# A gated cross-attention block with a ternary feed-forward layer: VectorE makes the second half's gated product before the sum of the exponentials

## The reference

```
h   = layernorm(x)
x   = x + tanh(g_xattn) * (softmax((h Wq)(ctx Wk)^T / 8) (ctx Wv) Wo + bo)      # 8 heads of 64
h   = layernorm(x)
g, u = bitlinear(h, w_gate), bitlinear(h, w_up)                                 # 512 -> 2048
x   = x + tanh(g_ffn) * bitlinear(relu(g)^2 * u, w_down)                        # 2048 -> 512
bitlinear(a, w) = act_quant(a) @ weight_quant(w).T
   act_quant: each row is scaled to 127 / max|row| and rounded; weight_quant: ternary, -1, 0 or 1 times a mean
```

## Time and profile before

| what | value |
|---|---|
| median of 3 runs | 1203.57 us (1203.33 to 1204.34) |
| the profiled execution: its own time | 1205.63 us |
| its span in the trace | 1203.7 us |
| granted TensorE clock over the span (1 is full speed) | 0.997 |
| TensorE busy with matrix products | 1181.2 us, 98% |
| VectorE busy | 1029.0 us, 85% |
| ScalarE busy | 870.7 us, 72% |
| GpSimd busy | 307.4 us, 26% |

### The profile page before, as it was taken

The page is one execution under the profiler, slowest core; times in us unless marked ns, Lnnn a source line. Parts: engine busy times, 40 slices in busy tenths (PEclk is TensorE's granted clock), DMA queues, the critical chain, the costliest instruction groups (busy, mean ns, idle before and its releaser), DMA issues.

```text
span 1203.7 us, 18706 instructions
## 1 busy us (share of the span) xinstructions
PE 1181.2 (98%) x5859; PEld 743.6 (62%) x5859; DVE 1029.0 (85%) x2123; ACT 870.7 (72%) x928; POOL 307.4 (26%) x313
## 2 busy tenths in 40 slices
PE   9998999999999999999999999999999999999997
PEld 7655566656656666666556656666665666566653
DVE  4888888888989888888988888889898888888876
ACT  4877767777877777677877766776787777677764
POOL 3231222222442222222432222222244222222200
PEclk9998999999999999999999999999999999999999
DMA  9796445444444464344444445444444444444432
GB/s 341 267 288 162 101 99 101 114 100 98 96 105 101 104 186 108 93 104 106 100 98 96 116 147 136 97 109 97 106 100 100 98 99 115 100 98 96 98 66 58
DMA packets 286268, 144.60 MB, mean 120 GB/s; under 512 B 254509, under 2 KB 254893, under 8 KB 283684
## 3 DMA queue, kind: packets, MB, share of 16 engines
q1 hardware_dynamic: 286240, 144.32, 47.0%
q10 hardware_dynamic: 4, 0.00, 0.0%
HBM read 57.86 MB, written 24.35 MB: 68 GB/s over the span
## 4 chain that ended last, share of the span: by engine, by line
PE 77%; DVE 11%; ACT 5%; issue 4%; DMA 3%; SPq 0%; POOL 0%; DVEq 0%; ACTq 0%; POOLq 0%
PE gu_ps L1000 30%; PE o_ps L970 16%; PE s_ps L66 14%; PE y_ps L1014 14%; DVE half_max L1249 2%; DVE staged L1243 2%; DMA v_scr<-x 2%; DMA w_down<-in_wu_t 1%; ACT x_marked L811 1%; DVE probs L1221 1%; DVE prob_sum L1225 1%; ACT v_sb L672 1%; PE gu_ps L1060 1%; ACT staged L785 1%; DVE stats L1278 1%
## 5 line engine op out<-in xcount | busy, mean ns | idle before, releaser
L1000 PE MATMUL gu_ps<-w_gate,xq_t 128*128 128x512 bf16 x1016 | 242.6, 382 | 12.5 <-DVE staged L1243 11.5
L1000 PE MATMUL gu_ps<-w_up,xq_t 128*128 128x512 bf16 x1024 | 242.5, 380 | 0.0
L1014 PE MATMUL y_ps<-w_down,hq_t 128*128 128x512 bf16 x1008 | 228.0, 379 | 1.4 <-DMA hq_t<-staged 1.3
L970 PE MATMUL o_ps<-v_sb,pt_high 128*128 128x512 f32 (+1 forms) x640 | 212.8, 413 | 0.0
L1243 DVE TENSOR_TENSOR staged<-staged,gu_ps 128x1024 f32<-128x1024 f32 x128 | 155.6, 1215 | 61.1 <-ACT staged L748 61.1
L66 PE MATMUL s_ps<-a_sb,xf_high 128*128 128x308 f32 x1024 | 187.3, 305 | 0.0
L610 POOL TENSOR_TENSOR rstd<-var_eps,neg_half 128x1 f32<-128x1 f32 x128 | 96.3, 752 | 310.6 <-DVE var_eps L1208 271.4
L1000 PEld LDWEIGHTS gu_ps<-w_up,xq_t 128*128 128x128 bf16 x1024 | 100.2, 98 | 121.8 <-issue 1.3
L1014 PEld LDWEIGHTS y_ps<-w_down,hq_t 128*128 128x128 bf16 x1008 | 98.3, 98 | 121.0 <-DMA hq_t<-staged 1.8
L1000 PEld LDWEIGHTS gu_ps<-w_gate,xq_t 128*128 128x128 bf16 x1016 | 94.0, 98 | 127.1 <-issue 15.9
L785 ACT ACTIVATE staged<-staged,h_scale 128x1024 f32<-128x1024 f32 x126 | 138.1, 1144 | 46.8 <-DVE h_scale L1263 46.5
(11 more groups left out here) (142 smaller groups left out, 1438.5 us busy)
## 6 DMA issues: line engine op xcount, KB each, us to landing
xf_sb<-in_x_feat SPq DMA_DIRECT2D x64, 256.0 KB, 2.7
x_sb<-in_x_tok SPq DMA_DIRECT2D x64, 256.0 KB, 2.9
y<-staged SPq DMA_DIRECT2D x64, 256.0 KB, 2.1
staged<-in_wg_t SPq DMA_DIRECT2D x4, 1024.0 KB, 9.8
staged<-in_wd_t SPq DMA_DIRECT2D x4, 1024.0 KB, 7.3
folded<-a_scr SPq DMA_DIRECT2D x3, 1232.0 KB, 5.6
v_scr<-x SPq DMA_DIRECT2D x12, 256.0 KB, 2.7
folded<-v_scr SPq DMA_DIRECT2D x3, 1024.0 KB, 7.7
```

The lines of the kernel that those rows point to most:

```text
L970: last = nc.tensor.matmul(o_ps[:, :], pt[0:rows, P * c:P * (c + 1)], v_sb[0:rows, v, c, :], start=(c == 0 and pt is pt_high and v == 0), s ...
L1000: last = nc.tensor.matmul(target[:, q, :], xq_t[:, s.par(0), c, :], w[:, c, cols], start=(c == 0), stop=(c == DC - 1))
L1014: last = nc.tensor.matmul(y_ps[:, :], hq_t[:, c, :], w_down[:, c, :], start=(c == 0), stop=(c == FC - 1))
```

## The change

In VectorE's `step`, `hidden_half(s, 1)` of tile t moves ahead of `sum_probs(s, 3)` of tile t+3. `top_half(s, 1)` and `hidden_scales` stay behind the sum. Nothing is added or removed.

```diff
                     if s.has(1):
                         hidden_unit_scale(s, 1)
+                    if s.has(0):
+                        hidden_half(s, 1)
                     if s.has(3):
                         sum_probs(s, 3)
                     if s.has(0):
-                        hidden_half(s, 1)
                         top_half(s, 1)
                         hidden_scales(s)
```

## The result

The changed kernel takes 1223.25 us (median of 5 runs, 1222.87 to 1224.94), the kernel before 1204.34 beside it (5 runs, 1203.33 to 1206.17). The ratio is 1.015, 95% interval 1.0138 to 1.0161: slower, by some 19 us. Forecast were 1220.4, and 1208 to 1230. TensorE is busy as long as before (1181.2 us there), and so it is idle longer.

What follows compares the result with a forecast made beforehand. TensorE, 17.28 us per tile, was taken as the bound; the free engines' loop becomes 16.84 - 0.65 + 1.27 = 17.46 and overtakes it. With first, split, load and end terms, 1203.57 + 16.8 = 1220.4 us, range 1208 to 1230.

Steps and rivals of the forecast that it cites:

- first interval: From the second-half product of tile 0 to the next tile's: 18.5 us, with tile 0's product 0.94 earlier.
- three value tiles, over the loop: Tiles where GpSimd splits the values: each 2.44 us over the free loop, on ScalarE's mark-to-shift path, 7.3 in all.
- three key tiles: Tiles where GpSimd splits the keys after a later `normalise`: scores about 0.9 us late, some 0.65 passed on, 2.0 in all.
- two load tiles: Tiles falling on the next batch's loads, where the planes' transpose comes late: 2.6 us for both, between 1 and 4.5.
- The loop of 16.84: The kernel before: time per tile through VectorE and ScalarE running freely, 0.44 us under TensorE's 17.28.
- The longer part: From second-half product to `mark_hidden`, which now waits behind ScalarE's planes: 4.66 us instead of 3.39, so 1.27 longer.
- The shorter part: From `shift_scores` to second-half product, which now waits for ScalarE's square: 2.69 us instead of 3.34, a gain of 0.65.
- TensorE's waits: At `attend` (L970), TensorE waits for `pt_low` (L1232), moved back 0.82 us against the product, in most tiles.
- The rule weighed: GpSimd and VectorE lock a shared SBUF port: `xq` costs 0.86 us more per value tile; mere sharing would give 1217.8.
- TensorE as the bound: Rival: the new loop stays under TensorE's 17.28 us per tile, about 1208.5 us in all; chance 0.06.
- the planes in time: Rival: ScalarE's planes are not late, `mark_hidden` comes at 4.22, loop 17.02, no change at 1203.5 us; chance 0.05.
- the steeper one: Rival: sum and `mark_hidden` start only after product and planes fully end; loop 17.69, 1234.0 us; chance 0.07.

Runs made afterwards that it cites:

- experiment 11: The changed kernel unaltered, measured again beside other runs on one chip: 1224.01 us, ratio 1.0157 to the kernel before.
- The first experiment: The changed kernel with GpSimd's `normalise` multiplying only the first of each head's 77 exponentials: 1211.22 us, ratio 1.005 to the kernel before.
- The third: The kernel before with the second-half product moved ahead of the sum in every second step only: 1210.78 us, ratio 1.0048.
- The sixth experiment: The changed kernel with `hidden_unit_scale` moved a step later, into VectorE's gap ahead of the first-half product: 1226.99 us, ratio 1.0185 to the kernel before.
- experiments 4: The kernel before with the three one-element instructions of `hidden_unit_scale` moved behind `hidden_scales`: 1212.3 us, ratio 1.0056.
- the seventh: The changed kernel with the sum moved further, behind `top_half` and `hidden_scales`: 1388.28 us, ratio 1.1525 to the kernel before.
- 8: The changed kernel with GpSimd splitting all five value chunks ahead of `normalise` instead of three: 1227.35 us, ratio 1.0184 to the kernel before.

## Why the prediction was right

The forecast of 1220.4 stands 2.9 below the median. Its steps against the changed kernel's trace, where both counted from the product of tile 0 to that of tile 60:

| step of the prediction | forecast | measured |
|---|---|---|
| sum, inverse, `normalise`, planes, `mark_hidden` after the product | 1.13, 1.95, 2.23, 3.48, 4.66 | 1.14, 1.96, 2.24, 3.49, 4.67 |
| ordinary interval | 17.46 | 17.43 (17.51 at every fourth) |
| first interval | 18.5 | 18.02 |
| three value tiles, over the loop | 2.44 each | 2.4 each |
| three key tiles | 0.65 each | 1.1 each |
| two load tiles | 2.6 | 0.8 (1.3 in experiment 11) |
| tile behind a value tile | none | 0.7 each |
| 60 intervals | 1060.5 | 1061.0 |
| behind tile 60 | 0.7 | 16.35 - 15.64 = 0.71 |

**One reading of the kernel before was too wide.** The loop of 16.84 was said to hold no instruction that waits for TensorE. VectorE's rows hold none, but ScalarE's relu of the second half did wait (timeline of ScalarE in the kernel before):

```profile
643.82 1.03 ACT L742 ACTIVATE staged<-gu_ps 128x1024 f32<-128x1024 f32 x1 [0.60 <-PE gu_ps L1000]
```

The 16.84 stands all the same: the square behind that relu ended at 646.49, and the product at 647.03 came straight behind the sum's inverse, with no idle time ahead of it.

**The longer part** is the step on which it all rested, and it held to 0.01 us. The first experiment shows the planes as its cause and not only their company. The third shows the threshold.

**The shorter part** was right too: the product waits for ScalarE's square, here 0.18 us where I expected some 0.3, and the distance from the shift to the product is 529.08 - 526.40 = 2.68, forecast 2.69. The sixth experiment shows that time freed on VectorE ahead of the product is worth nothing.

**Every fourth interval** is 0.08 longer. The trace says where: at the border of two rounds of four steps ScalarE's planes start 1.33 us after `normalise` and not 1.25 (timeline of ScalarE; `normalise` started at 513.81).

```profile
515.14 1.27 ACT L755 ACTIVATE planes<-probs 128x1280 int16<-128x1280 int16 x1 [3.60 <-POOL probs L615]
```

The kernel before has the same 0.08 at the same tiles, where it costs nothing. That it is the loop's branch is likely from its place, and not shown. Some 13 times 0.08 is 1.0 us which the prediction didn't have, and its 17.46 instead of 17.43 covered it.

**The key tiles** were sized too small, 0.65 against 1.1. The scores wait, and relu behind them, in the timelines of TensorE and ScalarE:

```profile
325.78 0.83 PE L66 MATMUL s_ps<-a_sb,xf_high 128*128 128x308 f32 x4 [1.00 <-POOL a_sb L598]
```

```profile
331.23 1.02 ACT L742 ACTIVATE staged<-gu_ps 128x1024 f32<-128x1024 f32 x1 [1.55 <-PE gu_ps L1000]
```

GpSimd started on the keys when it was expected, 318.78 - 315.37 = 3.41 after the product, but took 6.94 us for them, where the prediction carried over 6.49 (timelines of GpSimd, over all of it and over its end):

```profile
318.78 6.94 POOL L598 TENSOR_TENSOR a_sb<-folded,a_sb 128x616 fp32r<-128x616 f32 x4
```

```profile
323.76 1.96 POOL L598 TENSOR_TENSOR a_sb<-folded,a_sb 128x616 fp32r<-128x616 f32 x1
```

Each of its four instructions takes 1.5 us alone, and the one that meets `pt_low` takes 2.1, in both kernels. The fourth (the second row) took 1.96 instead of 1.53: VectorE's `unmark_hidden` now comes while the third is at work and ahead of the fourth, where it came during the fourth before. The keys were ready 10.35 after the product and not 9.9, so the scores began 10.41 after it, 1.43 later than in the kernel before where 0.9 was forecast, and 1.1 of that reached the product. The share that gets through was about right (0.65 of 0.9); the length of the split was the term that was too small.

**The tile behind a value tile** is a term that was missing. `normalise` stands between GpSimd's third and fourth chunk of the values, so a later sum makes the last chunks late (timeline of TensorE):

```profile
360.33 0.73 PE L970 MATMUL o_ps<-v_sb,pt_high 128*128 128x512 f32 x2 [1.57 <-POOL v_sb L605]
```

The last two chunks start 3.41 after the product instead of 1.34, and take 3.08 us instead of 2.51, as `pt_low` now starts beside them. The prediction followed `normalise` to the keys and not to the values. Together the missing 2.2 and the 1.3 too little for the keys stand against 1.8 too much for the load tiles and 0.5 for the first: the total was good in part because these cancel.

**The first interval** came out at 18.02. The product of tile 0 came 12.58 us after that of the tile's first half instead of 13.52, so 0.94 earlier, as forecast. But from it to `add_attention` it took 10.19 us instead of 10.67, and this is TensorE's clock, which the prediction did not look at. Before, TensorE waited 5.05 us for the product, and from 107 to 112 us, at work again, it was granted 0.50 of full speed. In the changed kernel it waited 4.14 us, had 1.00 before 107 us, 0.76, 0.50, 0.50 and 0.54 in the next four, and 1.00 from 111 us on. From the gate products to `attend` it took 4.95 us instead of 5.47.

**TensorE's waits** were expected "before L970 for L1232 in most tiles". The list names ten of them (3.2 us), and 23 waits of the weight load for "issue" at the same line. The starts show more than the list (timelines of TensorE and VectorE):

```profile
514.91 1.89 PE L1000 MATMUL gu_ps<-w_up,xq_t 128*128 128x512 bf16 x8
517.14 0.73 PE L970 MATMUL o_ps<-v_sb,pt_high 128*128 128x512 f32 x2 [0.33 <-DVE pt_low L1232]
```

```profile
516.13 0.82 DVE L1232 TENSOR_TENSOR pt_low<-probs_t,pt_high 128x640 fp32r<-128x640 f32 x1 [0.31 <-issue]
```

From the up products to `attend` it is 1.54 us in every ordinary tile of the kernel before. In the changed kernel, in the four tiles that end here, it is 1.54, 1.54, 1.74 and 2.23. TensorE runs two tiles of a round at its own pace and then stands ahead of `attend` in the other two, most of all at the border of two rounds, where `pt_low` itself starts 0.3 to 0.4 late. `attend` begins 0.14 to 0.19 us after `pt_low` has ended there. So the sign was right about the place and the releaser, and wrong about "most tiles": it is about half of them.

**The rule weighed**: in a value tile `xq` takes 1.27 us again, and the value tiles cost what was forecast with it. The trace agrees with the exclusive lock in the Trainium skill (SBUF — State Buffer, "SBUF: two separate sides"), and so do experiments 4, 7 and 8, the seventh above all, where the one that starts first keeps its time. What I didn't see is how much more than the one `xq` hangs on it.

**The rivals**: TensorE as the bound would have needed 17.28 in ordinary tiles; the planes in time, a `mark_hidden` at 4.22, of which only the first experiment comes near (4.17); the steeper one a loop of 17.69. None came. The median stands 2.9 over the forecast, of which 0.9 is in the span (17.7 instead of 16.8): 0.5 in the 60 intervals, 0.3 less because the start phase was shorter in that execution, and 0.7 behind VectorE's last instruction, where 3.3 us passed to the end instead of 2.6. That last is not the change's: the first experiment, with the new order, has 2.6 again. The other 2 are those by which I had moved the profiled execution's own time down to the median; the changed kernel's profiled execution stands at its median.

## What to carry to other kernels

When work on an engine in order is moved, ask what stands behind its consumer in the consumer's own queue. Here the sum's consumer was a chain over GpSimd to ScalarE, and the instruction that closes the loop stood behind it; the 0.65 us gained at one place of the loop cost 1.27 at another. Sum the loop through the free engines, from a tile that runs behind a stall, and compare it with the bound's time: under it a change costs nothing in ordinary tiles, over it every tile pays. And after such a move look at the few tiles that are unlike the others, since what starts a microsecond earlier or later there can meet another engine's long instruction.

## What the runs showed of the hardware

- A VectorE instruction on one element per partition with two tensors as its input took far longer while GpSimd worked on a long one: 0.92, 1.42, 1.45, 0.63 and 1.19 us instead of 0.15. That such a small one takes that long I had not expected. L1304, with one tensor as its data and the others as scalars, kept its 0.27 while GpSimd was at work.
- It works the other way round: GpSimd's `normalise` took 1.72 us instead of 1.22 when `pt_low` had begun 0.17 before it. When `normalise` had begun 0.35 before `pt_low`, it kept 1.21 and `pt_low` took 1.54.
- Wide ones lose as much: `pt_low` 1.86 and 1.88 instead of 0.82, `centred` 1.35 instead of 0.49. The reduction L1249 kept its 1.17 to 1.20 beside `normalise` and beside the split of the values.
- After a wait of TensorE the granted clock was sometimes 0.50 of full speed, the lower of its two levels (1.2 of 2.4 GHz), when it worked again: after 5.05 us in the first tile before and 4.14 us after, after 2.32 us in one tile of the third experiment and not after 2.33 in another. Eight matmuls then took 3.45 us instead of 1.89.
- At the border of two rounds of the loop ScalarE's planes started 0.08 us later behind `normalise`, and VectorE stood 0.31 us ahead of `pt_low` waiting for nothing that the trace shows, 13 times in either kernel.
